# A fused transformer block on one core: two query products instead of three, and the rotary swap by transfers

## What is computed

```python
def _rotate_half(x):                       # pairs of neighbours: (x1, x2) -> (-x2, x1)
    x1 = x[..., ::2]
    x2 = x[..., 1::2]
    return jnp.stack((-x2, x1), axis=-1).reshape(x.shape)
def _apply_rope(x, cos, sin):
    return x * cos + _rotate_half(x) * sin
...
q = _rms_norm(x @ w_qa, q_a_norm_w) @ w_qb          # 96 -> 16 heads of 128 + 64
q_nope, q_rope = (q[..., :D_NOPE], q[..., D_NOPE:])
q_rope = _apply_rope(q_rope, cos, sin)
k_rope = _apply_rope(k_rope[:, None], cos, sin)      # one for all heads
scores = jnp.einsum('bhsd,bhtd->bhst', q_full, k_full) * scale
attn = jax.nn.softmax(jnp.where(mask, scores, lowest), axis=-1)
out = jnp.einsum('bhst,bhtd->bhsd', attn, v)
```

## Time and profile before

| | us |
|---|---|
| median of 3 runs | 1255.79 |
| lowest, highest | 1254.54, 1256.06 |
| the profiled execution | 1254.86 |
| its span, first to last instruction | 1253.1 |
| busy: PE, PEld | 1146.3, 958.8 |
| busy: DVE, ACT, POOL | 846.8, 787.5, 690.3 |

### The profile page before, as it was taken

One profiled execution on the slowest core, in us unless ns is written; L12 is line 12 of the kernel. 1 busy time (PEld: TensorE's weight loads), 2 busy tenths in 40 slices (PEclk: granted clock), 3 DMA queues, 4 the chain that ended last, 5 costly groups with the idle time before them and its releaser, 6 DMA issues. The chain is left out here.

```text
span 1253.1 us, 27841 instructions
## 1 busy us (share of the span) xinstructions
PE 1146.3 (91%) x11372; PEld 958.8 (77%) x11372; DVE 846.8 (68%) x1900; ACT 787.5 (63%) x1166; POOL 690.3 (55%) x569
## 2 busy tenths in 40 slices
PE   2856899999999999999999999999999778989897
PEld 1744577888888888888888888888887667888886
DVE  2632876677676776777777677776675576767676
ACT  1254577777777878777787787877777532322222
POOL 0022366777777768686787776877777711202000
PEclk9876699999999999999999999999999879989998
DMA  9301110000100200100020020010000310000000
GB/s 277 95 1 48 29 44 18 2 18 25 38 19 2 62 2 19 44 19 19 2 62 18 2 61 2 19 44 19 18 2 1 114 57 1 1 18 1 18 18 17
DMA packets 57695, 39.91 MB, mean 32 GB/s; under 512 B 7744, under 2 KB 57152, under 8 KB 57408
## 3 DMA queue, kind: packets, MB, share of 16 engines
q1 hardware_dynamic: 51216, 33.94, 9.2%
q10 hardware_dynamic: 6352, 4.19, 1.4%
HBM read 33.66 MB, written 4.46 MB: 30 GB/s over the span
## 5 line engine op out<-in xcount | busy, mean ns | idle before, releaser
L669 POOL TENSOR_TENSOR pt_lo<-pt 128x1024 f16<-128x1024 f32 x192 | 370.5, 1939 | 181.5 <-ACT pt L726 181.2
L782 DVE TENSOR_REDUCE gates<-bank 128x1 f32<-128x512 f32 x384 | 261.6, 689 | 148.0 <-PE bank L849 145.1
L717 ACT ACTIVATE pair<-shift 128x1024 f32<-128x1024 f32 x256 | 263.7, 1030 | 12.2 <-ACT pt L730 0.4
L726 ACT ACTIVATE pt<-pair 128x1024 f32<-128x1024 f32 x192 | 196.2, 1022 | 108.3 <-PE pair L876 107.7
L891 PEld LDWEIGHTS bank<-values,pt 128*128 128x128 bf16 x2176 | 196.8, 98 | 80.1 <-issue 52.6
L891 PE MATMUL bank<-values,pt 128*128 128x65 f16 x2176 | 235.2, 194 | 6.0 <-DVE lat L808 5.1
L893 PE MATMUL bank<-values,pt 128*128 128x64 f16 x2176 | 231.8, 192 | 0.0
L895 PE MATMUL bank<-values,pt_lo 128*128 128x65 f16 x2176 | 230.8, 194 | 0.0
L675 POOL TENSOR_TENSOR pt_lo<-pt 128x512 f16<-128x512 f32 (+3 forms) x256 | 178.3, 722 | 45.0 <-ACT pt L730 44.9
L893 PEld LDWEIGHTS bank<-values,pt 128*128 128x128 bf16 x2176 | 202.0, 98 | 0.0
L895 PEld LDWEIGHTS bank<-values,pt_lo 128*128 128x128 f16 x2176 | 201.3, 97 | 0.0
(11 more groups left out here) (218 smaller groups left out, 2380.0 us busy)
## 6 DMA issues: line engine op xcount, KB each, us to landing
turn_by<-rope_cos_by_feature SPq DMA_DIRECT2D x64, 128.0 KB, 3.0
turn_by<-rope_sin_by_feature SPq DMA_DIRECT2D x64, 128.0 KB, 3.0
xs<-in_L_attn_x ACTq DMA_DIRECT2D x1, 2048.0 KB, 25.5
lat<-in_L_attn_w_o SPq DMA_DIRECT2D x1, 2048.0 KB, 26.6
xs_again<-in_L_attn_x SPq DMA_DIRECT2D x1, 2048.0 KB, 8.1
out<-xs_again SPq DMA_DIRECT2D x4, 512.0 KB, 2.8
lat<-in_L_wmod SPq DMA_DIRECT2D x1, 1536.0 KB, 16.3
lat<-in_L_attn_w_qb SPq DMA_DIRECT2D x1, 1152.0 KB, 8.0
```

Of the source, the lines that this page charges most:

```text
L669: pool.tensor_tensor(out=pt_lo[:, at].rearrange("p a n -> p (a n)"), in0=full, in1=cut(full), op=ALU.subtract).then_inc(low_ok, 1)
L717: act.activation(s_pair[u % 2][:, :, :], shift[:, item % SHIFTS:item % SHIFTS + 1, :].to_broadcast([P, 2, BW]), ACT.Copy).then_inc(seeded[ ...
L726: act.activation(pt[:, at], s_pair[u % 2][:, :, :], ACT.Exp).then_inc(exp_done, 1)
L782: dve.tensor_reduce(out=to, in_=of, axis=AXX, op=ALU.max).then_inc(work_seen["v"], 1)
```

## The change

- Product 2 is gone, with the third of the query weights that it needed (`wq_parts` and its SBUF copies shrink from 384 to 256 columns). The rotary features are now laid out as all even ones and then all odd ones, in the weights of the query, in the tables and in the key (`kk`, `krot`), so that the swap is an exchange of blocks of 32 partitions.
- One product now holds the rotary rows of both heads (product 0) and one the plain rows of both (product 1). A pair takes them in rounds r and r + 1.
- VectorE in round r: one scalar_tensor_tensor over 128 rows (times a sign per partition, times the sine, into the SBUF buffer `by_sin`), and two multiplications of 64 rows with the cosine. It no longer adds.
- SyncE then copies `by_sin` to `swapped` in four transfers of 32 partitions, each to the neighbouring block. It issues the tables of the next pair after that: 8 transfers of 32 partitions in place of 4 of 64, in one buffer in place of two. The weights come last in the queue.
- GpSimd in round r + 3 adds `swapped` to the two rotary parts (`query_sum`), waiting for the end of each.
- The high and low parts are made in round r + 5. `qf` has two buffers. The first product stands 8 rounds ahead of the first chunk in place of 6, so the first round numbers are 2 lower, and the first is -15. The number of shift buffers goes from 4 to 3.
- `prepare` has 4 pieces of rotary weights to move in place of 8, on ScalarE and on VectorE.

The core of the diff:

```diff
-PT_RING, SHIFTS, Q_SLOTS, MAXIMA = 4, 4, 3, 4
-AHEAD, PREP_AHEAD = 5, 6
+PT_RING, SHIFTS, Q_SLOTS, MAXIMA = 4, 3, 3, 4
+AHEAD, PREP_AHEAD = 5, 8
...
-PREP_AT = {r + n: (p, n) for p, r in enumerate(PREP_ROUND) for n in range(4)}
+PREP_AT = {r + n: (p, n) for p, r in enumerate(PREP_ROUND) for n in range(2)}
+SUM_AT = {r + 3: p for p, r in enumerate(PREP_ROUND)}
+SPLIT_AT = {r + 5: p for p, r in enumerate(PREP_ROUND)}
...
-        wq_dram = nc.dram_tensor("wq_parts", (2, NP, QL, 3 * P), F32, kind="Internal").ap()
+        wq_dram = nc.dram_tensor("wq_parts", (2, NP, QL, 2 * P), F32, kind="Internal").ap()
...
+                def tables(p):
+                    for n, name in enumerate(("cos_t", "sin_t")):
+                        of = k[name].rearrange("(i e) (j g p) -> e i j g p", e=2, j=BT, g=NG)[:, :, :, PAIRS[p][1], :]
+                        for half in range(2):
+                            for e in range(2):
+                                at = half * DR + e * (DR // 2)
+                                sp.dma_start(turn_by[at:at + DR // 2, n, :].rearrange("d (j p) -> d j p", j=BT),
+                                             of[(e + n) % 2]).then_inc(turn_in, 16)
+                def swap(p):
+                    wait_seen(sp, WORK[("q", p, 0)])
                     if p > 1:
                         sp.wait_ge(q_sum, 2 * p - 2)
+                    for at in range(0, P, DR // 2):
+                        of = at ^ (DR // 2)
+                        sp.dma_start(swapped[at:at + DR // 2, p % 2, :], by_sin[of:of + DR // 2, :]).then_inc(q_swapped[p % 2], 16)
+                weights(PAIRS[0][0])
+                tables(0)
+                for p in range(len(PAIRS)):
+                    swap(p)
+                    if p + 1 < len(PAIRS):
+                        tables(p + 1)
+                    if p + 1 < len(PAIRS) and PAIRS[p + 1][0] != PAIRS[p][0]:
+                        sp.wait_ge(work_done, WORK[("q", p, 1)] + 1)
+                        weights(PAIRS[p + 1][0])
...
+                def query_sum(p, r):
+                    if r >= 0:
+                        pool.wait_ge(low_ok, OPS[r + 1])
+                    if min(SPLIT_AT) < r:
+                        pool.wait_ge(q_lo_ok, 2 * sum(n < r for n in SPLIT_AT))
+                    pool.wait_ge(q_swapped[p % 2], 64 * (p // 2) + 64)
+                    for hd in range(2):
+                        pool.tensor_tensor(out=qf[ROT[hd], p % 2, hd, :], in0=swapped[ROT[hd], p % 2, :],
+                                           in1=qf[ROT[hd], p % 2, hd, :], op=ALU.add).then_inc(q_sum, 1)
+                        pool.wait_ge(q_sum, 2 * p + hd + 1)
...
+                def query_turn(p):
+                    n = WORK[("q", p, 0)]
+                    if p > 1:
+                        dve.wait_ge(q_lo_ok, 2 * p - 2)
+                    if p > 0:
+                        dve.wait_ge(q_swapped[(p - 1) % 2], 64 * ((p - 1) // 2) + 64)
+                    else:
+                        dve.wait_ge(sign_ok, 3)
+                    dve.wait_ge(turn_in, 128 * (p + 1))
+                    dve.wait_ge(work_done, n + 1)
+                    dve.scalar_tensor_tensor(out=by_sin[:, :], in0=work_of(n)[:, :], scalar=sign[:, :], in1=turn_by[:, 1, :],
+                                             op0=ALU.mult, op1=ALU.mult).then_inc(work_seen["v"], 1)
+                    for hd in range(2):
+                        dve.tensor_tensor(out=qf[ROT[hd], p % 2, hd, :], in0=work_of(n)[ROT[hd], :], in1=turn_by[ROT[hd], 0, :],
                                           op=ALU.mult).then_inc(work_seen["v"], 1)
```

150 lines of the change are left out of this document (61 added, 89 removed).

## The result

The changed kernel takes **1285.57 us** (median of 4 runs, 1283.27 to 1289.3) against 1255.17 for the kernel before in the same comparison: a ratio of 1.0245, interval 1.0219 to 1.027. It is 30 us slower where 13 us of gain were forecast, and 29.6 us above the upper end of the range (1256). The profiled execution took 1285.16, its span is 1283.4.

The account below looks back on a forecast made before the run. It took TensorE to bound the dense attention rounds: 20.6 us saved, less 3.0 (start), 2.4 (VectorE's turn) and 2.0 (queue), gave -13.2 and 1242.6 us; 8-in-10 range 1234 to 1256.

Parts of the forecast that it names:

- The third product, 20.6: TensorE's query products in the dense rounds: dropping the third saves 0.71 us in each of 29 pairs, 20.6 us.
- VectorE's turn, 2.4: Three VectorE operations hold a PSUM bank that a shift product wants: 0.3 us late in eight places, 2.4 us lost.
- The sum on GpSimd, 0: Two added sums a pair on GpSimd, 2.7 us, covered by short units: priced at 0, up to 1.3 us a pair.
- The queue, 2.0: SyncE's swap, tables and weights at six changes of heads: query products wait 0.3 us each, 2 us lost.
- The start, 3.0: Chains before round 0: it begins 4.1 us later, partly given back, net 3.0 us lost, bounds -2 and +9.
- S: Rival: GpSimd becomes late and low parts delay the weighing by 1.3 us in 29 pairs, 1280 us; chance 0.08.
- Q: Rival: SyncE's half-size transfers cost as much as whole ones, six weight waits of 2.0, 1255.6 us; chance 0.12.
- K: Rival: idle TensorE in the start keeps its clock at half for some 20 us longer, 1252 us; chance 0.06.
- C: Rival: all covered, no wait grows and the start is even, 1235.2 us; chance 0.12.
- All three signs of being wrong: TensorE idle over some 10 us in the middle, weighing waiting for low parts, or dense stretch beginning 10 us late.

Follow-up runs that it names:

- b1: Kernel before with the third query product made of one matmul in place of three: 1244.18 us against 1254.35, ratio 0.9916.
- m2: f2 with VectorE's turn cut to two operations, the cosine part being one 128-row multiplication: 1250.0 us, ratio 0.9957 to the kernel before.
- m0: Changed kernel with VectorE's turn of two operations in place of three as its only edit: 1268.6 us, ratio 1.0099 to the kernel before.
- e1: Changed kernel with the next head's weights issued ahead of the next tables on SyncE: 1278.5 us, ratio 1.0200 to the kernel before.
- f2: e1 with the sums moved from GpSimd to VectorE, behind the copy of the output bank: 1272.7 us, ratio 1.0145 to the kernel before.
- e2: Changed kernel with the sums moved from GpSimd to VectorE, ahead of the copy of the output bank: 1287.7 us, ratio 1.0268 to the kernel before.
- e4: Changed kernel without its swap transfers, so the result is not the block's: 1266.74 us, ratio 1.0104 to the kernel before.

## Why the prediction was wrong, step by step

**The third product, 20.6.** The count was right; that the whole of it comes off the end "as long as no other wait grows" was the condition that failed. Even in the kernel before only three quarters appear (b1). In m2, with the three causes gone, the dense rounds are 13.1 us shorter.

**VectorE's turn, 2.4: the step that failed.** The round behind it has 19.3 us of new waits, and a turn shorter by one operation gave 17.0 us of time back (m0). The prices were right (0.75 and 2 x 0.69 us against 0.70 and 2 x 0.69). I set the turn's end against one thing, the bank that the fourth use wants, found it 0.3 us late in eight places and called the rest covered by rounds of 2.9 us. At pair 9, my example, the turn begins 0.29 us behind the weighing (I had 0.17), ends 2.49 behind it (2.17), and the shift product starts at 2.54 where I had it wanted at 1.88: 0.66 late. Such a wait for the turn's end stands in 13 pairs. What I left out is the use behind it: the second query product takes the bank of the next chunk, whose maximum VectorE reduces only when the turn is done. In 24 pairs it starts right behind that maximum, in pair 7 at 3.14 us behind the weighing where a shift product at 2.58 would let it start at 2.81. So nothing covered the other pairs. The length of the turn was not new: in the kernel before VectorE's query work stood in three rounds of 0.7, 0.7 and 2.1 us, and the third ended at 2.44. New was that a shift product (25 of 28 pairs, 7 before) and a query product (all, none before) stand in the round behind it. The share of VectorE in a stretch, 73%, can't show this, and neither can its load in one round. The trace shows the waits and the runs show what a shorter turn gives; how much of the 17.0 us belongs to the held bank and how much to the late maximum, no run shows.

**The sum on GpSimd, 0.** The price per operation was right (1.34) and the share nearly (81% for 84%); the 0.69 us that I set beside it as the same shape is a 64-row operation, for 128 rows VectorE has 0.70. The cover was not: 13.3 us of waits, 15 start to start, at the changes of heads, where pairs stand four rounds apart and sums and low halves of two pairs meet a row of full units. I had checked the round of the sum and that of the halves for one pair alone. Moving the sums was worth 11.5 us of dense rounds (e1 to f2), given away again when they stood in front of the evacuation (e2).

**The queue, 2.0.** Six places, as said, but 10.1 us of waits and 7.1 us of time (e1). The swap issues take 0.6 us each and not the 0.31 of a weight issue, four of them going from 308.17 to 310.63; the tables take 0.58 there and not 0.46 on the average. Most of the table issues do start 0.47 apart, as estimated, but at pair 8 the last takes 1.16, and one such long one, of 1.2 to 1.8, stands in five of the seven changes of heads; why, the profile doesn't say. Together the second weight is issued 7.6 us behind the start of the swap, where I had 5.4.

**The start, 3.0.** In it 4.1 stood for the later beginning of round 0. That measured 8.3, and 1.6 more in the preparation. Against my times: turn of pair 1 at 131.9 for 129.3 (1.6 of preparation, 1.2 of swap issue), turn of pair 2 at 142.3 for 138.5 (1.2 more of swap issue), round 0 at 151.6 for 145.7 (2.1 more for the chunks and shifts behind that turn). Leaving the swap out gave 5.8 back (e4).

**The rivals.** S had the right side and part of the mechanism, low parts behind the sums, but in 29 pairs, with the turn at no loss; it was given 0.08. Q had the place and about the size of the weights' waits. None had what stands behind the turn in VectorE's queue. K did not come: the mean granted clock was 0.50, its lower level, from 120 up to 144 us in the kernel before and 0.76 from 144 to 148, and 0.50 up to 152 and 0.71 from 152 to 156 in the changed one, so the clock came back some 8 us later, with round 0, and not 20. C needed every wait covered. All three signs of being wrong came: more than 10 us of idle TensorE in the middle, weighings that wait for low parts, and dense rounds that begin 9.9 us late, just about the 10 named. Outside the range it came because every cover failed at once: 19.3 (turn), 10.1 (weights) and 15 (low parts) of waits and 9.9 of a later round 0 stand where the sum had 7.4 in all.

## What to carry to other kernels

Where work of several rounds is gathered into one, or moved to another, take its end and ask of every use in the round behind it what it waits for: the buffer that this work holds, and the operations queued behind it on the same engine. The share of a stretch hides that, and so does the load of one round. A wait that goes may only be the first of several that stand close behind, so try the removals together too. And freeing a buffer sooner is no gain if it is bought with more work on the engine that is late.

## What the runs showed of the hardware

- In the changed kernel the `spread` operation, two SBUF inputs, took 0.691 us at least and 2.392 at most over 64 of them, over 1 us in 21; in the kernel before in 6, with 2.391 at most. The multiplication with an input from PSUM, of 64 too, took 0.682 to 0.696. Of the two only the first was stretched, and at pair 6 the GpSimd operation beside it ran 2.34 for 1.90.
- In the changed kernel a 64x512 sum took GpSimd 1.286 us and a 128x512 subtraction 1.290 (medians of 64): half the partitions saved nothing.
- Four transfers of 64 KB from SBUF to SBUF took 2.4 to 2.5 us to issue on one queue. One of the same size from the tables took 0.47 in most places from one issue to the next, and now and then 1.2 to 1.9.
